# Four-head steps in latent attention, a later copy in the integer FFN, and a free bank for local attention's queries: one fused kernel on one core

## The chip, the core and the metric

The kernel runs on 1 core of one Trainium2 chip. Its time is device microseconds (us) from the start of the program to its end; less is better. The engines are TensorE (PE, with its weight loads shown as PEld), VectorE (DVE), ScalarE (ACT), GpSimd (POOL) and SyncE (SP, which only issues transfers here). They run side by side, each through its own list of instructions in order, and wait for one another on semaphores.

## The reference, cut to what matters

Four layers with float32 activations of 32 sequences x 256 tokens x 128 features; each layer is a layer norm, an attention branch `s`, an FFN branch `g`, and `x = x + s * silu(g)`. Three of the eight branches bear on the change:

```
# layer 0, attention: 8 query heads on 2 latent key/value heads, causal over 256 tokens
q = (x @ wq).reshape(Bq, Tq, N_KV, N_REP, HEAD_DIM)
k_lat = (x @ wk_down).reshape(Bq, Tq, N_KV, D_LAT)
v_lat = (x @ wv_down).reshape(Bq, Tq, N_KV, D_LAT)
scores = jnp.einsum('bqhrd,bkhd->bhrqk', q, k) * scale
probs = jax.nn.softmax(jnp.where(causal, scores, min), axis=-1)
y = jnp.einsum('bhrqk,bkhd->bqhrd', probs, v)
# layer 1, FFN: integer weights, hidden size 384
h = jax.nn.silu(x @ wg.T) * (x @ wu.T)
return h @ wd.T
# layer 3, FFN: two layers of windowed attention (8 heads of 64, window 64) and a gelu FFN
q, k = rotary_xpos(l2norm(q) * qs, l2norm(k) * ksc)
o = local_attention(q, k, v)
x = x + o @ wo
```

## The kernel before

Features lie on the 128 partitions, tokens along the rows. The program is a row of blocks; in each, every engine has a list written out in Python, and semaphores named after what was done (`scores`, `exps`, `turned_sb`) order the engines. `wait_ge(*S["exps"].at(i, n))` waits for the n-th exponential group of round i. PSUM is one tensor `ps` of 8 banks of 512 float32.

**Latent attention** (`latent_attention`) runs twice, for 16 sequences each, once with the transfers that scatter token rows to DRAM (`sorted_x`) and once with those that gather them. One sequence is four steps of two heads. A step's scores are three groups of matmuls into two banks (0 and 1, or 2 and 3 by turns): L573 and L576 are the score matmuls, each head in its own 32 rows of the array, L580 adds the causal mask. Then VectorE takes the row maxima (L750, L751), ScalarE the exponentials with their row sums (L712), TensorE turns the three 128-column blocks of each head (L589) into banks 4 and 5, VectorE copies them out (`probs_t`, L772), and `pe_mix` (L601) multiplies by the values into bank 6. Once a sequence come the reciprocals of the sums (L760), spread over the partitions by POOL (L677), TensorE (L611) and ScalarE (`inv_spread`, L724), the product `ot` (L765), the output projection (L623) with its copy (L739), and the projections k, q and v of sequences ahead (L617, L628), copied out by VectorE (k, L776) and ScalarE (q, L728, and v, L735). All of these use bank 7 in turn.

**Integer FFN** (`integer_ffn`): 16 chunks of 512 tokens, three hidden blocks f = 0, 1, 2 each. A step is a `down` matmul (L1312), one block of four transposes (L1288, L1296 or L1303, by f), an `up` matmul (L1323) and a `gate` matmul (L1328). Woven in is the next layer norm: `scale` (L1345) on ScalarE norms a chunk's rows, L1296 turns them back, and a ScalarE copy (L1360) puts them into `xn`; the silu of the gate (L1353) is ScalarE's too.

**Local attention** (`local_attention`), per layer 64 slots of 128 tokens. In slot k TensorE does the scores of k, the projections q and k of k + 3 and v of k + 1, transposes, the mix and the output of earlier slots. Seven of these results take banks 6 and 7 by turns, in the order of `MISC`; `pe_free` waits for whoever reads the result two places before. Bank 5 holds the mix (`attended` reads it), bank 4 the turned probabilities, banks 0 to 3 the scores.

Of the kernel before, what the change touches and what calls it, by code (L numbers as in the profile page):

```python
# [23 lines left out]
ALU = mybir.AluOpType  # L24
# [46 lines left out]
class Stage:  # L71
# [21 lines left out]
    "projected", "freed_act", "freed_dve", "scores", "masked", "rowmax", "exps", "turned", "turned_sb",  # L93
# [450 lines left out]
def latent_attention(nc, ps, m, w, first_pair, pairs, move, weights):  # L544
# [4 lines left out]
    with ExitStack() as mem:  # L549
# [5 lines left out]
        pr, nm, pt = buf("probs", P, 2, 2, W), buf("minus_max", P, 2, 2, 2), buf("probs_t", P, 4, 2, W)  # L555
# [7 lines left out]
        def pe_scores(pe, i, j):  # L563

            u, c, s = j % 8 // 4, j % 4 // 2, j % 2
            pe.wait_ge(*S["exps"].at(i, j - 2))
            if j % 4 == 0:
                pe.wait_ge(*S["k_sb"].at(i, j // 4))
                pe.wait_ge(*S["q_sb"].at(i, j // 4))
            b0 = 2 * s  # L570
            for e in range(2):
                rows = slice(32 * (2 * s + e), 32 * (2 * s + e) + 32)
                pe.matmul(ps[:, b0 + e, P:W], qt[rows, u, c, P:T], kt[rows, u, c, :], start=True, stop=False)  # L573
            for e in range(2):
                rows = slice(32 * (2 * s + e), 32 * (2 * s + e) + 32)
                pe.matmul(ps[:, b0 + e, 0:P], qt[rows, u, c, 0:P], kt[rows, u, c, 0:P], start=False, stop=False)  # L576
            for e in range(2):
                rows = slice(64 * e, 64 * e + 64)
                for h in range(2):
                    mm = pe.matmul(bank(ps, b0 + e, 3, P)[64 * h:64 * h + 64, ::2], one[rows, rows],  # L580
                                   hide[rows, h:h + 1].to_broadcast([64, 2, P]), start=False, stop=True)
            mm.then_inc(*S["scores"].inc)

        def pe_turn(pe, i, j):
            pe.wait_ge(*S["exps"].at(i, j))
            pe.wait_ge(*S["turned_sb"].at(i, j - 1))
            for e in range(2):
                for k in range(3):
                    mm = pe.transpose(ps[:, 4 + e, k * P:(k + 1) * P], pr[:, j % 2, e, k * P:(k + 1) * P], m["ident"][:])  # L589
            mm.then_inc(*S["turned"].inc)  # L590

        def pe_mix(pe, i, g):

            u, c = g % 4 // 2, g % 2
            pe.wait_ge(*S["turned_sb"].at(i, 2 * g + 1))
            pe.wait_ge(*S["v_sb"].at(i, g // 2))
            if c == 0:
                pe.wait_ge(*S["attended"].at(i, g // 2 - 1))
            for kb in range(2):
                for r in range(4):  # L600
                    mm = pe.matmul(ps[32 * r:32 * r + 32, 6, c * T + kb * P:(c + 1) * T], v[:, u, kb, c * LAT:(c + 1) * LAT],  # L601
                                   pt[:, (2 * g + r // 2) % 4, r % 2, kb * T:T + kb * P], start=(kb == 0), stop=(kb == 1))
            mm.then_inc(*S["mixed"].inc)

        def pe_spread(pe, i, n):
            pe.wait_ge(*S["widened"].at(i, n))
            if here(i, n + 2, 2):
                pe.wait_ge(*S["k_sb"].at(i, n + 2))
            for c in range(2):
# [22 lines left out]
        names = dict(copied=2, scores=8, rowmax=8, exps=8, turned=8, turned_sb=8, mixed=4, rowsum=2, widened=2, spread=2,  # L632
                     spread_sb=2, attended=2, q_ps=2, q_sb=2, k_ps=2, k_sb=2, v_ps=2, v_sb=2, o_ps=2, o_sb=2)
        with Stage(pairs, **names), Stage(1, moved0=TOK), nc.Block() as block:
            @block.tensor
            def _(pe):
                def body(i):
                    for t in range(8):
                        u, at = t // 4, t % 4
                        if t % 2 == 0 and here(i, t // 2 - 2, 4):  # L640
                            pe_mix(pe, i, t // 2 - 2)
                        if here(i, t + 1, 8):
                            pe_scores(pe, i, t + 1)
                        if here(i, t - 1, 8):
                            pe_turn(pe, i, t - 1)
                        if at == 0 and here(i, u - 1, 2):
                            pe_spread(pe, i, u - 1)
                        if at == 1 and here(i, u + 1, 2):
                            pe.wait_ge(*S["k_sb"].at(i, u + 1))
                            pe.wait_ge(*S["spread_sb"].at(i, u - 1))  # L650
                            pe_project(pe, i, u + 1, lambda c: wq[:, c], "q_ps")
                        if at == 2:
                            if here(i, u + 1, 2):
                                pe.wait_ge(*S["q_sb"].at(i, u + 1))
                            if here(i, u - 1, 2):
                                pe_out(pe, i, u - 1)
                            if here(i, u + 1, 2):
                                pe_v(pe, i, u + 1)
                        if at == 3 and here(i, u + 2, 2):
                            pe.wait_ge(*S["o_sb"].at(i, u - 1))  # L660
                            pe.wait_ge(*S["v_sb"].at(i, u + 1))
                            pe.wait_ge(*S["copied"].at(i, u + 2))
                            pe_project(pe, i, u + 2, lambda c: wk[:, c].rearrange("p r l -> p (r l)"), "k_ps")

                written_out(pairs, 1, 1, body)

            @block.gpsimd
            def _(pool):
# [3 lines left out]
                for i in range(-1, pairs + 1):  # L672
                    for u in range(2):
# [10 lines left out]
                        if here(i, u, 2):  # L684
                            for t in itertools.islice(tiles, TOK // (2 * pairs) - 1):
                                move(pool, t)
                            if here(i, u + 1, 2):
                                pool.wait_ge(*S["q_sb"].at(i, u + 1))
# [10 lines left out]
            def _(act):  # L699
                act.preload_act_table_set("exp_and_others")  # L700

                def exps(i, j):
                    u, c, s = j % 8 // 4, j % 4 // 2, j % 2
                    act.wait_ge(*S["rowmax"].at(i, j))
                    act.wait_ge(*S["turned"].at(i, j - 2))
                    if j % 4 == 0:
                        act.wait_ge(*S["rowsum"].at(i, j // 4 - 2))
                    for e in range(2):
                        head = 4 * c + 2 * s + e
                        for qb in range(2):  # L710
                            span = slice(qb * P, P + qb * T)
                            last = act.activation(pr[:, j % 2, e, span], ps[:, 2 * s + e, span], ACT.Exp,  # L712
                                                  bias=nm[:, s, qb, e:e + 1], accum_out=sums[:, u, qb, head:head + 1])
                    last.then_inc(*S["exps"].inc)

                def body(i):
                    for t in range(8):
                        u, at = t // 4, t % 4
                        if here(i, t, 8):
                            exps(i, t)  # L720
                        if at == 0 and here(i, u - 1, 2):
                            act.wait_ge(*S["spread"].at(i, u - 1))
# [1801 lines left out]
```

## Time and profile before

| | us |
|---|---|
| median of 3 runs (lowest to highest) | 2907.16 (2902.68 to 2909.36) |
| the profiled execution's own time | 2906.29 |
| its span in the trace | 2904.5 |
| TensorE busy | 2675.6 (92%) |
| VectorE busy | 2159.2 (74%) |
| ScalarE busy | 1934.7 (67%) |
| POOL busy | 1101.1 (38%) |

Busy time is the union of an engine's instructions in one profiled execution. Matmuls overlap in the array, so one that starts 0.05 us after another may last 0.2. A share over the whole span averages stages that differ, and what counts is read stage by stage. Times in the trace are us from the start of the span.

### The profile page before, as it was taken

Reading aid. Unit: us, or ns where it says so; the run is one execution under the profiler, and the core shown is the slowest. Engines: PE = TensorE matmul, PEld = TensorE weight load, DVE = VectorE, ACT = ScalarE, POOL = GpSimd, SP = SyncE. Lnnn points to the kernel's source line nnn. Section 1 sums busy time; section 2 is a strip of 40 time slices with the busy share of each in tenths; the row PEclk is TensorE's granted clock in tenths of the full one; section 3 lists DMA queues with packets and bytes.
Section 4 is the critical chain, followed back from the end, with each engine's and each line's share of the span. In section 5 each row is a group of like instructions: output and inputs, shape, how many; then the busy total and the mean of one; then the engine's idle time right before and its main releaser. Section 6 shows DMA issues by size and latency. Waiting matters only on the chain. (4 is left out here: it accounts for less than half of the span.)

```text
span 2904.5 us, 62166 instructions
## 1 busy us (share of the span) xinstructions
PE 2675.6 (92%) x21644; PEld 1785.4 (61%) x21644; DVE 2159.2 (74%) x3766; ACT 1934.7 (67%) x5521; POOL 1101.1 (38%) x1260
## 2 busy tenths in 40 slices
PE   7799999997889979888879999998998999999898
PEld 4577897774554434345547777776444777777644
DVE  4577565776675669856769999997447999999676
ACT  4366665666764544344369999997437999999744
POOL 0233343331004543310045555554215555555431
PEclk9699998998999989989989999999998999999999
DMA  4200121000000000030000000000000000000000
GB/s 147 77 23 21 52 68 30 22 22 12 9 17 0 1 0 1 10 74 9 20 9 2 2 2 2 2 2 10 12 1 10 2 2 2 2 2 2 2 22 37
DMA packets 83170, 53.92 MB, mean 19 GB/s; under 512 B 28848, under 2 KB 75568, under 8 KB 82864
## 3 DMA queue, kind: packets, MB, share of 16 engines
q1 hardware_dynamic: 78768, 41.56, 5.1%
q0 software_dynamic: 4096, 8.40, 1.0%
q8 instruction: 178, 2.92, 0.4%
q14 instruction: 128, 1.05, 0.1%
HBM read 31.59 MB, written 18.35 MB: 17 GB/s over the span
## 5 line engine op out<-in xcount | busy, mean ns | idle before, releaser
L2124 ACT ACTIVATE probs<-banks,minus_max,rnorm 128x128 f32<-128x128 f32 x1024 | 460.0, 469 | 4.3 <-DVE minus_max L2220 4.3
L1996 PE MATMUL banks<-weights,hf 128*128 128x512 f32 x768 | 431.1, 645 | 24.4 <-POOL hf L336 13.5
L2039 POOL TENSOR_TENSOR qk_cross<-qk_raw,rope_scaled 128x512 f32<-128x512 f32 x256 | 325.9, 1274 | 25.5 <-ACT qk_raw L2157 11.5
L2049 POOL TENSOR_TENSOR qk_rot<-qk_rot,rnorm 128x512 f32<-128x512 f32 x128 | 133.5, 1043 | 291.8 <-DVE qk_rot L2253 283.3
L2124 ACT ACTIVATION_READ_ACCUMULATOR probs<-banks,minus_max,rnorm 128x1 f32 x1024 | 222.6, 217 | 0.0
L712 ACT ACTIVATE probs<-banks,minus_max 128x128 f32<-128x128 f32 (+1 forms) x512 | 207.9, 425 | 13.1 <-DVE minus_max L751 13.1
L2200 DVE COPY probs_t<-banks 128x512 f32<-128x512 f32 x256 | 175.9, 687 | 54.5 <-PE banks L1974 53.9
L1974 PEld LDWEIGHTS banks<-ident,probs 128*128 128x128 f32 x1024 | 126.8, 140 | 134.4 <-issue 134.4
L2246 DVE TENSOR_TENSOR qk_rot<-qk_raw,rope_scaled 128x512 f32<-128x512 f32 x256 | 175.8, 727 | 0.0
L2234 DVE TENSOR_REDUCE sumsq<-qk_sq 128x16 f32<-128x1024 f32 x128 | 154.8, 1209 | 26.9 <-issue 19.9
L2005 PE MATMUL banks<-ident,qk_rot 128*128 128x128 f32 x1024 | 159.6, 279 | 10.0 <-DVE qk_rot L2253 4.9
L2253 DVE TENSOR_TENSOR qk_rot<-qk_rot,qk_cross 128x1024 f32<-128x1024 f32 x128 | 161.4, 1261 | 4.4
L2216 DVE TENSOR_REDUCE minus_raw<-banks 128x8 f32<-128x1024 f32 x128 | 155.5, 1215 | 7.6 <-PE banks L1966 7.6
L1974 PE MATMUL banks<-ident,probs 128*128 128x128 f32 x1024 | 153.9, 273 | 6.0 <-DVE probs_t L2200 5.8
L1996 PEld LDWEIGHTS banks<-weights,hf 128*128 128x128 f32 x768 | 117.8, 193 | 53.1 <-POOL hf L336 15.1
L2439 DVE SCALAR_TENSOR_TENSOR qk_rot<-banks,b1t,qk_rot 128x512 f32<-128x512 f32 x96 | 71.9, 749 | 104.9 <-ACT qk_rot L2392 91.0
L1988 PE MATMUL banks<-v_tok,probs_t 128*64 128x64 f32 x3072 | 148.7, 226 | 0.0
L2005 PEld LDWEIGHTS banks<-ident,qk_rot 128*128 128x128 f32 x1024 | 114.8, 142 | 42.2 <-issue 39.3
L1988 PEld LDWEIGHTS banks<-v_tok,probs_t 128*64 128x64 f32 x3072 | 130.9, 138 | 11.8 <-issue 10.2
L750 DVE TENSOR_REDUCE minus_max<-banks 128x2 f32<-128x256 f32 x128 | 54.4, 425 | 111.2 <-PE banks L580 111.2
L2090 PE MATMUL banks<-ot,weights 128*128 128x128 f32 x1024 | 135.5, 275 | 0.0
L2138 ACT ACTIVATE qk_sq<-qk_raw 128x1024 f32<-128x1024 f32 x128 | 134.2, 1048 | 0.1
(354 smaller groups left out, 6985.2 us busy)
## 6 DMA issues: line engine op xcount, KB each, us to landing
sorted_x<-zero_rows SPq DMA_DIRECT2D x10, 512.0 KB, 6.0
rows_in<-sorted_x SPq DMA_DIRECT2D x18, 256.0 KB, 3.1
sorted_y<-rows_out SPq DMA_DIRECT2D x18, 256.0 KB, 2.4
x_res<-in_x SPq DMA_DIRECT2D x8, 512.0 KB, 6.7
out_x<-x_res SPq DMA_DIRECT2D x16, 256.0 KB, 2.0
w1b<-in_L_ffn_w SPq DMA_DIRECT2D x8, 256.0 KB, 3.9
s_branch<-in_L_ffn_w SPq DMA_DIRECT2D x8, 256.0 KB, 5.8
w1g<-in_L_ffn_W SPq DMA_DIRECT2D x8, 256.0 KB, 3.0
```

The lines of the kernel that those rows point to most:

```text
L712: last = act.activation(pr[:, j % 2, e, span], ps[:, 2 * s + e, span], ACT.Exp, bias=nm[:, s, qb, e:e + 1], accum_out=sums[:, u, qb, head: ...
L1974: mm = pe.transpose(ps[:, 4, n * P:(n + 1) * P], pr[:, k % 2, 4 * h + n], m["ident"][:])
L1988: mm = pe.matmul(ps[64 * w:64 * w + 64, 5, at], pt[:, h, n * P + 64 * w:n * P + 64 * w + 64], vm[:, at] if tb and not w else va[:, k % 4, ...
L1996: pe.matmul(ps[:, misc(k, j)], hf[:, n // 2 % 2, 0, n % 2 * P:(n % 2 + 1) * P], wqkv[:, w:w + QW], start=True, stop=True).then_inc(*S[name ...
L2005: mm = pe.transpose(ps[:, misc(k, j), c * P:(c + 1) * P], st[:, n % 4, first:first + P], m["ident"][:])
L2039: return pool.tensor_tensor(by_half(tw[:, n, at]), by_half(qk[:, n, at])[:, :, ::-1, :], tab[:, n, 2 * w + 1].rearrange("p (a d) -> p a d" ...
L2124: last = act.activation(pr[:, k % 2, head], ps[:, 2 * (k % 2) + par, c * P:(c + 1) * P], ACT.Exp, scale=rn[:, k % 4, head:head + 1], bias= ...
L2200: dve.tensor_copy(pt[:, h], ps[:, 4]).then_inc(*S["turned_sb"].inc)
L2216: dve.tensor_reduce(nr[:].rearrange("p (b c) -> p b c", b=2), ps[:, 2 * (k % 2):2 * (k % 2) + 2].rearrange("p b (c t) -> p b c t", c=4), A ...
L2234: dve.tensor_reduce(ss[:], by_head(sq[:]), AX.X, ALU.add).then_inc(*S["sumsq"].inc)
L2246: last = dve.tensor_tensor(by_head(st[:, n, at]), by_head(qk[:, n % 2, at]), tab[:, n % 2, 2 * w:2 * w + 1].to_broadcast([P, HEADS, DH]), ...
L2253: dve.tensor_tensor(st[:, n], st[:, n], tw[:, n % 2], ALU.add).then_inc(*S["rotated"].inc)
```

## The change

Three edits in one.

1. *Latent attention* goes in steps (slots) of four heads. A slot fills banks 0 to 3 with one set of scores, each head in one of the four 32-row groups; the four heads' twelve blocks are turned in three groups of four, each a whole bank, and ScalarE copies the first (`lead_sb`), VectorE the other two. To make up, ScalarE takes the k copy, and VectorE those of `inv_spread`, v and s. POOL's transfers, three and then one per sequence, become one, two and one, with waits for `turned_sb` between them.
2. *Integer FFN*: ScalarE's copy of the normed rows to `xn` moves from f = 1 to f = 2, ahead of `scale`.
3. *Local attention*: q is projected into bank 5, between `attended` and the next mix, and is no longer in `MISC`, which has six entries now. Some waits that others imply are gone.

```diff
-        pr, nm, pt = buf("probs", P, 2, 2, W), buf("minus_max", P, 2, 2, 2), buf("probs_t", P, 4, 2, W)
+        pr, nm, pt = buf("probs", P, 2, 4, W), buf("minus_max", P, 2, 2, 2, 2), buf("probs_t", P, 2, 4, W)
...
+        def pe_scores(pe, i, g):
+
+            u, c = g % 4 // 2, g % 2
+            pe.wait_ge(*S["exps"].at(i, g - 1))
...
+            for r in range(4):
+                rows = slice(32 * r, 32 * r + 32)
+                pe.matmul(ps[:, r, P:W], qt[rows, u, c, P:T], kt[rows, u, c, :], start=True, stop=False)
...
+        def pe_turn(pe, i, g, t):
+            if t == 0 and not here(i, g + 1, 4):
+                pe.wait_ge(*S["exps"].at(i, g))
+            if t == 2:
+                pe.wait_ge(*S["lead_sb"].at(i, g))
+            else:
+                pe.wait_ge(*S["turned_sb"].at(i, 2 * (g - 1) + t))
+            for k in range(4):
+                mm = pe.transpose(ps[:, 4 + (g + t) % 2, k * P:(k + 1) * P], blocks(pr, g, t)[:, k * P:(k + 1) * P],
+                                  m["ident"][:])
             mm.then_inc(*S["turned"].inc)
...
+                            move(pool, next(tiles))
+                            if here(i, 2 * u - 1, 4):
+                                pool.wait_ge(*S["turned_sb"].at(i, 2 * (2 * u - 1) + 1))
+                            for t in itertools.islice(tiles, TOK // (2 * pairs) - 2):
                                 move(pool, t)
-                            if here(i, u + 1, 2):
-                                pool.wait_ge(*S["q_sb"].at(i, u + 1))
+                            pool.wait_ge(*S["turned_sb"].at(i, 2 * (2 * u) + 1))
                             move(pool, next(tiles))
...
+                    if here(i, g - 1, 4):
+                        act.wait_ge(*S["turned"].at(i, 3 * (g - 1)))
+                        act.wait_ge(*S["mixed"].at(i, g - 3))
+                        act.activation(blocks(pt, g - 1, 0), ps[:, 4 + (g - 1) % 2], ACT.Copy).then_inc(*S["lead_sb"].inc)
+                    if here(i, g, 4):
+                        exps(i, g)
...
                     if f == 0 and 0 <= c - 1 < R:
                         branch(c - 1)
+                    if f == 2 and 0 <= c - 3 < R:
+                        act.wait_ge(*S["copied"].at(0, c - 3))
+                        act.activation(m["xn"][:, tokens(c - 3)], ps[:, ROWS_AT], ACT.Copy).then_inc(*S["normed"].inc)
                     if f == 2 and 0 <= c - 2 < R:
                         scale(c - 2)
-                    if f == 1 and 0 <= c - 3 < R:
-                        act.wait_ge(*S["copied"].at(0, c - 3))
-                        act.activation(m["xn"][:, tokens(c - 3)], ps[:, ROWS_AT], ACT.Copy).then_inc(*S["normed"].inc)
...
-MISC = [("qt_sb", 1), ("added", -3), ("q_sb", 3), ("kt_sb", 1), ("k_sb", 3), ("v_sb", 1), ("ot_sb", -2)]
-QT_AT, OUT_AT, Q_AT, KT_AT, K_AT, V_AT, OT_AT = range(7)
+MISC = [("qt_sb", 1), ("added", -3), ("kt_sb", 1), ("k_sb", 3), ("v_sb", 1), ("ot_sb", -2)]
+QT_AT, OUT_AT, KT_AT, K_AT, V_AT, OT_AT = range(6)
...
+        def pe_project_q(pe, i, k):
+            n = k + 3
+            if here(i, k - 2):
+                pe.wait_ge(*S["attended"].at(i, k - 2))
+            else:
+                pe.wait_ge(*S["q_sb"].at(i, n - 1))
+            pe.wait_ge(*S["copied"].at(i, n // 2))
+            pe.matmul(ps[:, 5], hf[:, n // 2 % 2, 0, n % 2 * P:(n % 2 + 1) * P], wqkv[:, 0:QW], start=True, stop=True)\
+                .then_inc(*S["q_ps"].inc)
```

In the middle of latent attention TensorE's list was, for somewhat more than two heads (`kt,qt` are the scores, `hide` the masks, `probs` the transposes, `v_tok` the mix, `wk_lat` and `wq_lat` projections):

```order
L573 MATMUL banks<-kt,qt 128x256 x2
L576 MATMUL banks<-kt,qt 128x128 x2
L580 MATMUL banks<-hide,ident_bf 64x2x128 x4
L589 MATMUL banks<-ident,probs 128x128 x6
L617 MATMUL banks<-xf,wk_lat 128x256 x2
L601 MATMUL banks<-probs_t,v_tok 32x256 x4
L601 MATMUL banks<-probs_t,v_tok 32x128 x4
```

Of the change, one slot and the start of the next:

```order
L575 MATMUL banks<-kt,qt 128x256 x4
L578 MATMUL banks<-kt,qt 128x128 x4
L583 MATMUL banks<-hide,ident_bf 64x2x128 x8
L595 MATMUL banks<-ident,probs 128x128 x4
L623 MATMUL banks<-ident,inv_wide 128x128 x4
L595 MATMUL banks<-ident,probs 128x128 x8
L629 MATMUL banks<-xf,wq_lat 128x256 x2
L609 MATMUL banks<-probs_t,v_tok 32x256 x4
L609 MATMUL banks<-probs_t,v_tok 32x128 x4
```

Scores come once for four heads instead of twice, and the transposes in fours. ScalarE's list in the same place, of the change, with the semaphores each row waits for (L743 copies q, L747 is the new copy of the first turned bank, L731 the exponentials):

```order
L743 ACTIVATE qt<-banks 128x512 [waits q_ps]
L747 ACTIVATE probs_t<-banks 128x512 [waits mixed,turned]
L731 ACTIVATE probs,row_sums<-banks,minus_max 128x128 [waits rowmax,turned]
L731 ACTIVATE probs,row_sums<-banks,minus_max 128x256
L731 ACTIVATE probs,row_sums<-banks,minus_max 128x128
L731 ACTIVATE probs,row_sums<-banks,minus_max 128x256
L731 ACTIVATE probs,row_sums<-banks,minus_max 128x128 [waits rowmax]
```

The copy of the turned bank stands between a slot's scores and its exponentials. In the integer FFN, ScalarE's list for one chunk before:

```order
L1353 ACTIVATE silu_gate<-banks 128x512
L1338 ACTIVATE gate<-banks 128x512
L1365 ACTIVATE s_branch<-banks,weights 128x512
L1353 ACTIVATE silu_gate<-banks 128x512
L1360 ACTIVATE xn<-banks 128x512
L1353 ACTIVATE silu_gate<-banks 128x512
L1345 ACTIVATE ln_rows<-banks,ln_shift,ln_scale 128x128 x4
```

And of the change:

```order
L1376 ACTIVATE silu_gate<-banks 128x512
L1361 ACTIVATE gate<-banks 128x512
L1388 ACTIVATE s_branch<-banks,weights 128x512
L1376 ACTIVATE silu_gate<-banks 128x512 x2
L1381 ACTIVATE xn<-banks 128x512
L1368 ACTIVATE ln_rows<-banks,ln_shift,ln_scale 128x128 x4
```

The third silu has moved ahead of the copy to `xn`. In local attention, TensorE's projections q, k and v of one slot before, with what they wait for and what stands between them:

```order
L1996 MATMUL banks<-weights,hf 128x512 [waits copied,qt_sb]
L1974 MATMUL banks<-ident,probs 128x128 [waits turned_sb,exps]
L2005 MATMUL banks<-ident,qk_rot 128x128 [waits unit,added]
L1996 MATMUL banks<-weights,hf 128x512 [waits copied,q_sb]
L1996 MATMUL banks<-weights,hf 128x512 [waits copied,kt_sb]
```

And of the change:

```order
L2023 MATMUL banks<-weights,hf 128x512 [waits copied,attended]
L1995 MATMUL banks<-ident,probs 128x128 [waits exps]
L2038 MATMUL banks<-ident,qk_rot 128x128 [waits unit,qt_sb]
L2029 MATMUL banks<-weights,hf 128x512 [waits added]
L2029 MATMUL banks<-weights,hf 128x512 [waits kt_sb]
```

The order of the work is the same; q waits for the reader of bank 5, k for the reader of the output, v as before.

## Rows read from the trace of the kernel before

**Rows 1.** Stretches of the span, busy us (instructions): PE, PEld, DVE, ACT, POOL; clock.

```profile
478.00:486.00 8.00, 8.00 (x42) 6.50 (x43) 3.57 (x6) 4.48 (x21) 0.94 (x1) 0.50 0.03 8
486.00:657.00 171.00, 171.00 (x1695) 129.78 (x1695) 122.30 (x205) 111.56 (x487) 65.53 (x83) 1.00 0.09 23
1600.00:1900.00 300.00, 298.81 (x3642) 220.52 (x3639) 281.15 (x431) 284.00 (x898) 174.13 (x180) 1.00 0.01 2
```

**Rows 2.** Time line, latent attention, TensorE: start, us, engine, line, instructions.

```profile
212.21 0.70 PE L573 MATMUL banks<-kt,qt 32*128 32x256 f32 x4
213.06 0.30 PE L580 MATMUL banks<-hide,ident_bf 64*64 64x256 bf16 x4
213.30 0.88 PE L589 MATMUL banks<-ident,probs 128*128 128x128 f32 x6
...
214.97 0.86 PE L601 MATMUL banks<-probs_t,v_tok 128*32 128x256 f32 x16
215.76 0.70 PE L573 MATMUL banks<-kt,qt 32*128 32x256 f32 x4
```

**Rows 3.** The same time line, VectorE and ScalarE; in brackets idle time before.

```profile
213.42 0.42 DVE L750 TENSOR_REDUCE minus_max<-banks 128x2 f32<-128x256 f32 x1 [0.44 <-PE banks L580]
213.76 0.68 DVE L751 TENSOR_REDUCE minus_max<-banks 128x2 f32<-128x512 f32 x1
214.36 0.95 DVE L772 COPY probs_t<-banks 128x768 f32<-128x768 f32 x1
215.07 0.60 ACT L728 ACTIVATE qt<-banks 128x512 f32<-128x512 f32 x1 [0.55 <-PE banks L617]
215.57 0.36 ACT L712 ACTIVATE probs<-banks,minus_max 128x128 f32<-128x128 f32 x1
...
219.49 0.37 ACT L712 ACTIVATE probs<-banks,minus_max 128x128 f32<-128x128 f32 x1
...
222.67 0.21 ACT L712 ACTIVATION_READ_ACCUMULATOR probs<-banks,minus_max 128x1 f32 x1
```

**Rows 4.** Time line, first latent stage: its first and fourteenth `ot`, its last copy.

```profile
127.97 0.69 DVE L765 TENSOR_TENSOR ot<-banks,inv_spread 128x512 f32<-128x512 f32 x1 [0.59 <-PE banks L601]
...
291.25 0.69 DVE L765 TENSOR_TENSOR ot<-banks,inv_spread 128x512 f32<-128x512 f32 x1 [0.59 <-PE banks L601]
...
311.91 0.38 ACT L739 ACTIVATE s_branch<-banks 128x256 f32<-128x256 f32 x1 [2.70 <-PE banks L623]
```

**Rows 5.** Integer FFN: time line of one chunk; last, waits (total, times, longest).

```profile
932.61 1.02 PE L1312 MATMUL banks<-hid,w_deq 128*128 128x512 f32 x2
933.47 0.60 PE L1296 MATMUL banks<-ident,ln_rows 128*128 128x128 f32 x4
933.91 1.02 PE L1323 MATMUL banks<-xn,w_deq 128*128 128x512 f32 x2
934.11 0.60 ACT L1360 ACTIVATE xn<-banks 128x512 f32<-128x512 f32 x1 [4.08 <-PE banks L1296]
...
935.24 1.13 PE L1328 MATMUL banks<-xn,w_deq 128*128 128x512 f32 x2 [0.31 <-ACT silu_gate L1353]
...
943.73 0.60 ACT L1360 ACTIVATE xn<-banks 128x512 f32<-128x512 f32 x1 [4.08 <-PE banks L1296]
...
PE banks L1328 <- ACT silu_gate L1353: 3.8, 12, 0.3
```

**Rows 6.** Time line, local attention, one slot: projections and the copies they wait for.

```profile
1702.13 0.60 ACT L2133 ACTIVATE qt<-banks 128x512 f32<-128x512 f32 x1
...
1702.82 1.08 PE L1996 MATMUL banks<-weights,hf 128*128 128x512 f32 x2
...
1703.74 0.60 PE L1974 MATMUL banks<-ident,probs 128*128 128x128 f32 x4
...
1705.30 0.60 ACT L2153 ACTIVATE kt<-banks 128x512 f32<-128x512 f32 x1
...
1705.99 1.09 PE L1996 MATMUL banks<-weights,hf 128*128 128x512 f32 x2
```

More of the change, by code:

```diff
@@ L561, in here @@
             return there(i, n, per, pairs)
[L563 to L589, printed above, removed]
+        def blocks(x, g, t):
+            return x[:, g % 2].rearrange("p h w -> p (h w)")[:, 4 * t * P:4 * (t + 1) * P]
+        def pe_scores(pe, i, g):
+            u, c = g % 4 // 2, g % 2
+            pe.wait_ge(*S["exps"].at(i, g - 1))
+            if c == 0:
+                pe.wait_ge(*S["k_sb"].at(i, g // 2))
+                pe.wait_ge(*S["q_sb"].at(i, g // 2))
+            for r in range(4):
+                rows = slice(32 * r, 32 * r + 32)
+                pe.matmul(ps[:, r, P:W], qt[rows, u, c, P:T], kt[rows, u, c, :], start=True, stop=False)
+            for r in range(4):
+                rows = slice(32 * r, 32 * r + 32)
+                pe.matmul(ps[:, r, 0:P], qt[rows, u, c, 0:P], kt[rows, u, c, 0:P], start=False, stop=False)
+            for s in range(2):
+                for e in range(2):
+                    rows = slice(64 * e, 64 * e + 64)
+                    for h in range(2):
+                        mm = pe.matmul(bank(ps, 2 * s + e, 3, P)[64 * h:64 * h + 64, ::2], one[rows, rows],
+                                       hide[rows, h:h + 1].to_broadcast([64, 2, P]), start=False, stop=True)
+                mm.then_inc(*S["scores"].inc)
@@ L667, in _ @@
+                written_out(pairs, 1, 1, lambda i: [slot(i, g) for g in range(4)])
             @block.gpsimd
@@ L744, in _ @@
+                written_out(pairs, 1, 1, lambda i: [slot(i, g) for g in range(4)])
             @block.vector
             def _(dve):
[L746 to L752 removed]
@@ L778, in _, with rowmax, turned @@
-                written_out(pairs, 1, 1, body)
+                def rowmax(i, g, s):
+                    dve.wait_ge(*S["scores"].at(i, 2 * g + s))
+                    dve.wait_ge(*S["exps"].at(i, g - 2))
+                    for qb in range(2):
+                        last = dve.tensor_reduce(nm[:, g % 2, s, qb], ps[:, 2 * s:2 * s + 2, qb * P:P + qb * T], AX.X,
+                                                 ALU.max, negate=True)
+                    last.then_inc(*S["rowmax"].inc)
+                def turned(i, g, t):
+                    dve.wait_ge(*S["turned"].at(i, 3 * g + t))
+                    if t == 1:
+                        dve.wait_ge(*S["mixed"].at(i, g - 2))
+                    dve.tensor_copy(blocks(pt, g, t), ps[:, 4 + (g + t) % 2]).then_inc(*S["turned_sb"].inc)
@@ L779, in latent_attention @@
+                written_out(pairs, 1, 1, lambda i: [slot(i, g) for g in range(4)])
         S["loaded"].base += 16 * len(weights)
```

215 lines of the change are left out of this document (103 added, 112 removed).

## The prediction

> **What bounds the kernel now.** I read the table of stretches first, then the time line inside each of the three stages that the diff touches, then the waits. The three stages are bound in three different ways.
>
> Latent attention (two stages of 16 sequences each). In a steady stretch of 171.00 us TensorE is busy for 171.00 us at the full granted clock, 2.4 GHz [rows 1]. The multiplication `ot` comes 13 intervals after its first occurrence at 291.25, so one sequence takes (291.25 - 127.97) / 13 = 12.56 us [rows 4]. For two heads TensorE needs 1.09 us for the scores (212.21 to 213.30), of which 0.85 are the score matmuls and the rest the masks; six transposes take 0.88 to their end; `pe_mix` takes 0.79 (214.97 to 215.76) [rows 2]. VectorE waits for TensorE here [rows 3], and ScalarE is busy for 111.56 of the 171.00 us [rows 1]. So only TensorE's instructions count.
>
> Integer FFN. Here the bound is a stall, not work. ScalarE stands 4.08 us in front of its copy to `xn`, waiting for the transposes of L1296; the silu that is queued behind the copy comes late, and TensorE's next gate matmul, which could start at 933.91 + 0.86 = 934.77, starts at 935.24 [rows 5]. A 512-column float32 matmul takes 0.86 (932.61 to 933.47) and a block of four transposes 0.44 (933.47 to 933.91), so a chunk is 9 x 0.86 + 3 x 0.44 = 9.06 us of TensorE, and its period is 943.73 - 934.11 = 9.62 [rows 5]. The loss is 0.56 a chunk, and TensorE was caught by that silu 12 times [rows 5].
>
> Local attention (two layers of 64 slots). TensorE is busy 298.81 of 300 us, VectorE 281.15, ScalarE 284.00 [rows 1]. All three are nearly full, so only small things are to be had. The q projection takes 0.92 (1702.82 to 1703.74), where the same matmul takes 0.86 elsewhere [rows 6, 5]: it waits for ScalarE's copy `qt`, which ends at 1702.13 + 0.60 = 1702.73, and comes with no time left to load the second half of the weights ahead.
>
> **The change, part by part: latent attention.** The four heads of a step now sit in four row groups, so what ran twice for two heads runs once for four. Scores for four heads cost 1.09 plus the second set of masks, which I put at 0.11 (an estimate: half of the 0.21 that 256 of the 0.86 us' 512 columns take in one of two passes, since the masks are bfloat16), 1.20 instead of 2.18. That is 0.98 per slot off TensorE, about 2 us of the 12.56 per sequence, and it ceases to be the bound.
>
> What is late next: the score banks are no longer doubled. All four are filled by one step, so `pe_scores` of slot g waits for the last exponential of slot g - 1, and behind that wait the whole TensorE queue stands. The ring, counted from the first score matmul: VectorE's first reduction starts at 1.21 (212.21 to 213.42) [rows 2, 3]; two reductions end at 1.21 + 0.34 + 0.68 = 2.23 [rows 3]. ScalarE meanwhile has the new `lead` copy: its four transposes start at 1.20 and end some 0.66 later (0.88 for six), so it starts near 1.89, and the next ScalarE instruction comes 0.50 behind such a copy (215.07 to 215.57) [rows 2, 3]. The exponentials therefore start at 2.39, not at 2.23. Four heads of them take 222.67 + 0.21 - 219.49 = 3.39 [rows 3], until 5.78, and a hand-over to TensorE about 0.05 to 0.1: **5.87 a slot**. A second ring goes through VectorE: 1.21, four reductions (2 x (0.34 + 0.60) = 1.88, as consecutive starts stand), then the copy of `inv_spread`, now VectorE's (0.60), two `probs_t` copies (0.60 and, to the end, 0.68), 0.05, and the mix with its 0.79 in front of the next scores: 5.81 [rows 2, 3]. In the other slot v and s (the shorter copies) replace that one. Both rings lie so close that one waits for the other now and then; I take 5.9, 11.8 a sequence, 0.76 less than now.
>
> Over 13 intervals that is 9.9 a stage. The end gives some back. Now the stage ends 311.91 + 0.38 - 291.25 = 21.04 after its last regular `ot` [rows 4]; after the change three slots follow that point (17.5 to the last exponential), and then transposes, lead copy, third transposes, copy, mix, `ot`, projection and copy in a row, 6.8: 24.3, so 3.2 worse. The start I leave at nothing: TensorE does less, but in the first two slots it must wait some 3 us for exponentials. There it ran at a granted 0.50 (1.2 GHz) though never idle [rows 1], and I can't read when the clock rises; bounds plus and minus 3. Sum: 9.9 - 3.2 = 6.7 a stage, **13.4** for two.
>
> What the trace does not show is four row groups at once. Two at once cost no more than one would ([rows 2]: the second of a pair hides). Bounds: 0, or, if the groups go two by two, the 0.85 again less the change of tile shape, about 0.75 a slot. Four column groups at once, in the mix, take 0.79 for eight matmuls [rows 2]; that is nearest in kind, so I take 0. The Trainium skill ("TensorE: Matmul & The Clock Gate", Part 3, measured speedup against the span model) gives four row tiles 3.07 times one, not four; the four would take 1.30 times one, and by that the slot would be an estimated 6.1 and the forecast 2891 instead of 2879. No row here shows four, so it is a rival below.
>
> The spread transfers (POOL) I cost at nothing: POOL is busy 65.53 of 171.00 us with its moves and copies [rows 1], and the only thing that waits for it is `pe_spread`, through `inv_wide`, which comes after 1.2 us of scores and four transposes. Where a move is still running then, that cover is gone, and a slot grows by up to one POOL instruction, 65.53 / 83 = 0.79 us on the mean [rows 1].
>
> **Integer FFN.** The copy now follows the silu of f = 2, so ScalarE's wait for L1296 holds up only the copy and `scale`, which has to wait for `ln_shift` anyway. The silu has its gate long before, and TensorE finds `act_a` done. Period 9.06: 12 x 0.56 = 6.7; I take **6.5**. Behind the copy `scale` now starts 0.5 after the transposes' end, and the next chunk's silu follows with about 2 us to spare for its `down` matmul. That cover hides it.
>
> **Local attention.** Nothing is added or taken out; q moves from banks 6 and 7 to bank 5, and waits. The q projection waits for `attended` (VectorE, long done) instead of the `qt` copy: 0.92 becomes 0.86, **0.06 a slot**. The k projection waited for the q copy, and now waits for `added` instead. I give that nothing: the v projection still waits for the `kt` copy (1705.30 + 0.60 = 1705.90, v starts 1705.99) [rows 6], which stands on ScalarE behind the q copy and two exponentials, as before. What k gains, v waits longer. 0.06 x 124 full slots = **7.4**. Bounds: 0, if another ring (VectorE is 94% full [rows 1]) takes over, and 0.18 a slot, 22, if k and v have an excess of the same size and both lose it.
>
> **Sum.** 13.4 + 6.5 + 7.4 = 27.3 off the profiled execution's own 2906.29 us, which is 0.87 below the median: 2879.
>
> **The rivals.** *Four row groups overlap only in part* (their weight loads stand in line): a quarter of the 0.75 between the bounds, 0.2 more a slot. A stage has about 29 slots that count (13 x 2 + 3), so 5.8 a stage and 2891. For it: four groups load eight weights where two load four. Against it: the mix loads for four groups within its 0.79 [rows 2]. The rule of the Trainium skill above (Part 3 of that page) would make this the likely case; the trace bears out only pairs.
>
> *Two by two*, the case on the other side: slot 5.87 + 0.75 = 6.6, 29 x 0.7 = 20 a stage more than forecast, 41 in all: 2920, slower. It decides from a slot of 6.4 on, where latent attention loses what the other two parts gain. Against it: tiles in other shapes run four at a time here.
>
> *The two small edits do nothing*: the FFN's stall turns up behind `scale`, and VectorE's ring binds local attention. 2879 + 14 = 2893. For it: VectorE and ScalarE are 94% and 95% busy there [rows 1]. Against it: the FFN's stall is one wait with one cause.
>
> *More than forecast*: k's and v's excess in local attention falls too, 15 more, 2864; or the start of latent attention gains 3 a stage.
>
> **How the numbers follow.** Forecast 0.50 (its own range 2868 to 2889), partial overlap 0.18, small edits nothing 0.08, more 0.14, two by two 0.07, the rest a mixture near no change. What is within 0.2% (5.8 us) can't be told from no change. Faster by more: 0.87; same 0.05; slower 0.08. From 2857 to 2897 the first four cases are nearly all held, with the bounds of the start and of local attention.
>
> **What would show it.** Right: `ot` every 11.8 us; TensorE about 90% busy in latent attention and waiting before the scores for ScalarE's `probs`; the `xn` copy's wait no longer followed by a late silu, chunks at 9.06; q at 0.86, v still above 0.9, slots 0.06 shorter. Wrong: scores for four heads much above 1.2, or a long wait for VectorE's `probs_t` in front of the mix, either of which makes the slot longer than 6.1; a `kt` copy that comes earlier than I reckon; or half clock reaching into the steady part.

## The result, and the profile after

2865.93 us (median of 4 runs, 2861.49 to 2867.06), against 2905.41 for the kernel before: a ratio of 0.9861, 95% interval 0.9848 to 0.9874. The time fell by some 40 us where 27 were forecast; the profiled spans are 2904.5 and 2864.5. The 40 us, read from how much earlier the same instruction starts in the two traces:

| part | forecast | measured |
|---|---|---|
| latent attention, up to the first `ot` | 0 (plus and minus 3 a stage) | -3.4 and -5.3 |
| latent attention, 13 intervals | -9.9 a stage | -10.3 and -10.0 |
| latent attention, end | +3.2 a stage | +4.6 and +4.0 |
| integer FFN | -6.5 | -7.1 |
| local attention, first slots (a layer's first projection to its fifth `qt` copy) | not looked at | -4.9 and -5.8 |
| local attention, full slots (from there to the last `qt` copy) | -7.4 for both layers | -1.6 and -1.8 |
| local attention, ends | not looked at | +1.7 and +1.0 |

Minus is faster. The rest, about 1, is small differences between the stages.

**Latent attention.** The time line of VectorE has the first and the fourteenth `ot` and the last copy of both stages:

```profile
124.53 0.69 DVE L779 TENSOR_TENSOR ot<-banks,inv_spread 128x512 f32<-128x512 f32 x1 [1.06 <-PE banks L609]
...
277.50 0.69 DVE L779 TENSOR_TENSOR ot<-banks,inv_spread 128x512 f32<-128x512 f32 x1 [1.06 <-PE banks L609]
...
302.67 0.42 DVE L795 COPY s_branch<-banks 128x256 f32<-128x256 f32 x1 [1.22 <-PE banks L635]
...
478.54 0.69 DVE L779 TENSOR_TENSOR ot<-banks,inv_spread 128x512 f32<-128x512 f32 x1 [1.06 <-PE banks L609]
...
631.83 0.69 DVE L779 TENSOR_TENSOR ot<-banks,inv_spread 128x512 f32<-128x512 f32 x1 [1.06 <-PE banks L609]
...
656.44 0.42 DVE L795 COPY s_branch<-banks 128x256 f32<-128x256 f32 x1 [1.91 <-PE banks L635]
```

(277.50 - 124.53) / 13 = 11.77 a sequence, where [rows 4] give 12.56; 25.6 from the last regular `ot` to the end, where it was 21.04. One slot on TensorE and ScalarE:

```profile
212.63 0.71 PE L575 MATMUL banks<-kt,qt 32*128 32x256 f32 x8
213.17 0.40 PE L578 MATMUL banks<-kt,qt 32*128 32x128 f32 x8
213.50 0.41 PE L583 MATMUL banks<-hide,ident_bf 64*64 64x256 bf16 x8
213.84 0.66 PE L595 MATMUL banks<-ident,probs 128*128 128x128 f32 x4
...
214.54 0.60 ACT L747 ACTIVATE probs_t<-banks 128x512 f32<-128x512 f32 x1 [1.57 <-PE banks L595]
...
215.03 0.36 ACT L731 ACTIVATE probs<-banks,minus_max 128x128 f32<-128x128 f32 x1
...
218.10 0.25 ACT L731 ACTIVATION_READ_ACCUMULATOR probs<-banks,minus_max 128x1 f32 x1
...
218.53 0.71 PE L575 MATMUL banks<-kt,qt 32*128 32x256 f32 x8
```

Scores of four heads take 213.84 - 212.63 = 1.21; the exponentials start 2.40 behind the first score (forecast 2.39), and the next scores come after 5.90. Eight score matmuls in four row groups take 0.71 where four in two take 0.70 [rows 2]. From two groups to four nothing is lost. One group alone stands in no row. With half of the 0.86 of a 512-column matmul [rows 5], 0.43, as an estimate for one, four in 0.54 (212.63 to 213.17) would be 3.2 times one. The Trainium skill ("TensorE: Matmul & The Clock Gate", Part 3, measured speedup against the span model) gives 3.07 times for four row tiles; the estimate is near it, and no run here tests it.

**The granted clock** by stretches of latent attention's second start and steady part, the integer FFN and local attention (columns as in [rows 1]):

```profile
450.30:463.70 13.40, 11.38 (x44) 7.03 (x44) 2.24 (x5) 3.75 (x9) 3.82 (x6) 0.50 0.06 15
463.70:467.10 3.40, 1.05 (x21) 0.82 (x24) 0.00 (x0) 2.88 (x13) 0.00 (x0) 0.99 0.00 0
467.20:470.60 3.40, 3.40 (x23) 3.11 (x16) 2.60 (x6) 1.96 (x8) 0.00 (x0) 0.50 0.02 5
...
470.00:640.00 170.00, 157.28 (x1792) 118.76 (x1792) 121.17 (x244) 123.46 (x519) 68.79 (x86) 1.00 0.09 24
905.00:965.00 60.00, 60.00 (x200) 30.35 (x199) 42.20 (x158) 31.09 (x64) 38.76 (x41) 1.00 0.00 1
1570.00:1870.00 300.00, 298.25 (x3672) 218.30 (x3671) 283.51 (x432) 284.97 (x901) 174.08 (x181) 1.00 0.01 2
```

TensorE now waits in latent attention (157.28 of 170.00) and is full in the integer FFN. There the copy still waits, and delays no silu: the chunk is 938.37 - 929.33 = 9.04, forecast 9.06.

```profile
929.33 0.60 ACT L1381 ACTIVATE xn<-banks 128x512 f32<-128x512 f32 x1 [3.71 <-PE banks L1319]
...
938.37 0.60 ACT L1381 ACTIVATE xn<-banks 128x512 f32<-128x512 f32 x1 [3.71 <-PE banks L1319]
```

**Local attention, a full slot** on TensorE, from the q projection to the v projection:

```profile
1668.59 1.02 PE L2023 MATMUL banks<-weights,hf 128*128 128x512 f32 x2
1669.45 0.60 PE L1995 MATMUL banks<-ident,probs 128*128 128x128 f32 x4
1669.89 0.60 PE L2038 MATMUL banks<-ident,qk_rot 128*128 128x128 f32 x4
1670.33 1.02 PE L2029 MATMUL banks<-weights,hf 128*128 128x512 f32 x2
1671.19 0.60 PE L1995 MATMUL banks<-ident,probs 128*128 128x128 f32 x4
1671.67 1.13 PE L2029 MATMUL banks<-weights,hf 128*128 128x512 f32 x2
1672.63 0.38 PE L2140 MATMUL banks<-ident,attended_tok 128*128 128x128 f32 x2
```

q takes 1669.45 - 1668.59 = 0.86 (0.92 before), as forecast. k takes 1671.19 - 1670.33 = 0.86 (0.94 before), but the turn behind it 0.48 (0.44 before), and v 0.96 (0.93 before): what k gains v waits, as forecast. Starts of the `qt` copy, before (the one behind that of [rows 6], and the next) and after:

```profile
1710.55 0.60 ACT L2133 ACTIVATE qt<-banks 128x512 f32<-128x512 f32 x1
1718.87 0.60 ACT L2133 ACTIVATE qt<-banks 128x512 f32<-128x512 f32 x1
...
1667.90 0.60 ACT L2165 ACTIVATE qt<-banks 128x512 f32<-128x512 f32 x1 [0.17 <-PE banks L2038]
1676.26 0.60 ACT L2165 ACTIVATE qt<-banks 128x512 f32<-128x512 f32 x1 [0.19 <-PE banks L2038]
1684.58 0.60 ACT L2165 ACTIVATE qt<-banks 128x512 f32<-128x512 f32 x1 [0.16 <-PE banks L2038]
```

They stand 8.36 and 8.32 apart by turns, where it was 8.42 and 8.32: every second slot gained nothing.

### The profile page after: what moved, and what is told of

Its sections match the earlier page's. It is cut to its first block and busy times, and to the rows that moved or that the text cites. A ratio compares the mean times of both kernels' runs of the same rounds, so it can differ in the third digit from the quotient of the medians.

```text
span 2864.5 us, 61209 instructions
## 1 busy us (share of the span) xinstructions
PE 2606.9 (91%) x21644; PEld 1734.9 (61%) x21644; DVE 2145.7 (75%) x3830; ACT 1946.8 (68%) x5521; POOL 1103.3 (39%) x1260
## 5 line engine op out<-in xcount | busy, mean ns | idle before, releaser
L2029 PE MATMUL banks<-weights,hf 128*128 128x512 f32 x512 | 276.8, 623 | 5.0 <-ACT kt L2185 5.0
L731 ACT ACTIVATE probs<-banks,minus_max 128x128 f32<-128x128 f32 (+1 forms) x512 | 206.6, 437 | 5.2 <-DVE minus_max L759 5.0
L759 DVE TENSOR_REDUCE minus_max<-banks 128x2 f32<-128x256 f32 (+1 forms) x256 | 124.9, 551 | 61.6 <-PE banks L583 61.6
L2023 PE MATMUL banks<-weights,hf 128*128 128x512 f32 x256 | 135.2, 611 | 13.6 <-POOL hf L336 13.6
```

Of the source, the lines that this page charges most:

```text
L731: last = act.activation(pr[:, g % 2, 2 * s + e, span], ps[:, 2 * s + e, span], ACT.Exp, bias=nm[:, g % 2, s, qb, e:e + 1], accum_out=sums[ ...
L2029: pe.matmul(ps[:, misc(k, j)], hf[:, n // 2 % 2, 0, n % 2 * P:(n % 2 + 1) * P], wqkv[:, w:w + QW], start=True, stop=True).then_inc(*S[name ...
```

## The experiments

A kernel's ratio is to the kernel before, run on the same chip.

**One part at a time** (three kernels: before, with the diff's part and nothing else).

> The kernel before with only the integer FFN's copy moved. Theory: the stall of 0.56 us a chunk is gone, chunks come every 9.06, and the time falls by 6.5 to 8 us against the kernel before (ratio about 0.9975). Rival: the stall turns up again behind the copy, chunk at 9.62 or near it, no change. The starts of the local layers should show TensorE's clock rising as in the kernel before, some 20 us after the layer's first matmuls; if it rises much earlier here too, the rise differs from one execution to the next and is no effect of the change.

0.9974 (0.9964 to 0.9984). From the integer FFN's end on its trace is 7 us ahead; its local layers start as before, first intervals of the `qt` copy 8.05, 7.61 and 8.16 (8.23, 7.61 and 8.16 in the kernel before).

> The kernel before with only local attention's part. Theory A: half of the slots gain 0.05 to 0.06 us (q at 0.86) and the other half, which POOL's two copies to v_mixed hold at 8.32, gain nothing: 1.75 us a layer, 3.5 in all, and the clock rises earlier at the start of both layers, 3.6 and 5.7 us more: 2905 - 12.5 = 2893. Theory B: the earlier rise is chance; then 3.5 alone, 2902. Theory of the prediction: 0.06 in every slot, 7.4, 2898.

0.9966 (0.9954 to 0.9978), 9.9 us. The interval rules out theory B, but holds A's 12.5 and the prediction's 7.4; the slots are A's: first intervals 6.40, 7.25, 7.51, then 8.36 and 8.32. A's reason for the starts, the clock, is put to the test in the next run but one.

> The kernel before with only latent attention's part. Theory A: 13 intervals x 0.79 = 10.2 a stage less, the end 4 to 4.5 worse, the start 3.4 and 5.3 better because TensorE's clock rises sooner: about 20 less in all, 2885. Theory B: the earlier rise is chance or comes from elsewhere: 12 less, 2893. In both, one sequence takes 11.77.

0.9937 (0.9923 to 0.9950), 18 us: theory A in size (20), and B's 12 is outside. The three parts add up to 0.9877, just above the interval of the whole (0.9848 to 0.9874); with their own intervals the two agree.

**q waits again, in bank 5.**

```diff
                 pe.wait_ge(*S["attended"].at(i, k - 2))
             else:
                 pe.wait_ge(*S["q_sb"].at(i, n - 1))
+            if here(i, k + 1):
+                pe.wait_ge(*S["qt_sb"].at(i, k + 1))
```

> The changed kernel, in which the q projection stays in bank 5 but waits for ScalarE's copy of the turned queries again. Theory: the gain of a slot comes from the wait alone and not from the bank: q goes back to 0.92 us, the slots that had 8.36 go to 8.42, and the time rises by 3 to 4 us to about 2869.5. If the bank itself were worth something, q would stay at 0.86 or the time would not rise. The starts of the layers keep their earlier rise of the clock, since in the first slots the wait is not there.

0.9904 (0.9889 to 0.9919): by the ratios 12 us of the gain gone, not 3 to 4. Full slots are at 8.43 and 8.33, as expected, but the first layer's first intervals are back at 8.64, 7.63, 8.17, for this wait is there in the first slots too. TensorE there, second and third slot of the first layer:

```profile
1451.97 0.66 PE L2040 MATMUL banks<-ident,qk_rot 128*128 128x128 f32 x4
1453.36 1.10 PE L2025 MATMUL banks<-weights,hf 128*128 128x512 f32 x2 [0.73 <-issue]
...
1458.78 0.66 PE L2040 MATMUL banks<-ident,qk_rot 128*128 128x128 f32 x4
1461.01 1.10 PE L2025 MATMUL banks<-weights,hf 128*128 128x512 f32 x2 [1.57 <-issue]
```

And in the changed kernel:

```profile
1452.82 0.66 PE L2038 MATMUL banks<-ident,qk_rot 128*128 128x128 f32 x4
1453.31 1.02 PE L2023 MATMUL banks<-weights,hf 128*128 128x512 f32 x2
...
1459.23 0.66 PE L2038 MATMUL banks<-ident,qk_rot 128*128 128x128 f32 x4
1459.84 1.10 PE L2023 MATMUL banks<-weights,hf 128*128 128x512 f32 x2
```

In a full slot eight output matmuls (0.89) stand between the query transposes and q, and cover the copy `qt`. In a layer's first slots there is no output yet, and q stands until the copy is done, 0.73 and 1.57 here. So most of the gain of the starts is this wait: from a layer's first projection to its fifth `qt` copy the kernel before takes 44.64 and 45.35, the change 39.73 and 39.59, and this run 43.51 and 42.71. It is not the whole. The first copy comes 10.62 and 11.09 behind the first projection in this run too (10.63 and 10.62 in the change, 12.22 and 12.23 before); and the clock has a part in the second layer, as the next run shows.

**q waits in full slots only** (the same, with `here(i, k - 3) and` ahead of the condition).

> The changed kernel, in which the q projection waits for ScalarE's copy of the turned queries only from the fourth slot of a layer on, where an output matmul stands between the two. Theory: the first slots keep their 3.4 to 5 us a layer (first intervals 6.4, 7.2, 7.5 as in the change), the full slots lose 0.06 and 0.01 by turns, 2 us a layer: 4 us slower than the change, ratio to before 0.9875. Rival (the gain of the starts is the clock's and comes and goes): the first intervals of a layer are not those of the change, ratio 0.990 or 0.986.

0.9878 (0.9861 to 0.9894). Time, full slots (8.43 and 8.33) and the first layer's first intervals (6.51, 7.24, 7.51) are as the theory has them. The second layer's are 7.35, 7.24 and 7.51, where the change has 6.30, 7.23 and 7.51: there the rival has a part. Its first 18 us, in the change and in this run (columns as in [rows 1]):

```profile
2150.50:2168.50 18.00, 13.55 (x68) 6.75 (x69) 9.84 (x12) 8.97 (x17) 9.29 (x9) 0.83 0.00 1
...
2148.70:2166.70 18.00, 14.62 (x61) 6.90 (x62) 8.22 (x11) 8.12 (x15) 8.83 (x9) 0.65 0.00 1
```

The waits of these slots are the same; the mean granted clock is 0.83 in one and 0.65 in the other, and up to the fifth `qt` copy they take 39.59 and 41.12. The second layer of the run with local attention alone takes 41.13. So some 1.5 of the 5.8 that the second layer's start gained go with the clock of the one execution, and not with the wait.

**The lead copy on VectorE.**

```diff
-                        act.activation(blocks(pt, g - 1, 0), ps[:, 4 + (g - 1) % 2], ACT.Copy).then_inc(*S["lead_sb"].inc)
...
                     if here(i, g - 1, 4):
+                        dve.tensor_copy(blocks(pt, g - 1, 0), ps[:, 4 + (g - 1) % 2]).then_inc(*S["lead_sb"].inc)
                         turned(i, g - 1, 1)
```

> The changed kernel, in which VectorE and not ScalarE copies the first of the three turned banks in latent attention. Theory: both engines' rings were close (5.87 and 5.81 us a slot); without the copy ScalarE's ring is 5.71, but VectorE's has one more copy of 0.60, 6.4 in the slots with the copy of the spread sums and about 6.3 in the others; so ot comes every 12.7 us in place of 11.77, and with 29 slots a stage the time rises by some 28 us, 2894. Rival (ScalarE's ring alone decides): a slot loses the 0.17 by which the copy delays the exponentials, ot every 11.4, 10 us faster, 2856.

1.0047 (1.0031 to 1.0064): 53 us slower than the change, `ot` every 13.45. The sign is the theory's, the size is not. From the time line of one slot:

```profile
211.15 0.71 PE L575 MATMUL banks<-kt,qt 32*128 32x256 f32 x8
...
213.51 0.37 ACT L731 ACTIVATE probs<-banks,minus_max 128x128 f32<-128x128 f32 x1 [2.48 <-DVE minus_max L755]
...
214.84 0.68 DVE L796 COPY probs_t<-banks 128x512 f32<-128x512 f32 x1
...
215.58 0.66 PE L595 MATMUL banks<-ident,probs 128*128 128x128 f32 x4 [1.69 <-DVE probs_t L796]
...
216.27 0.69 DVE L763 COPY probs_t<-banks 128x512 f32<-128x512 f32 x1 [0.15 <-PE banks L595]
...
217.11 0.86 PE L609 MATMUL banks<-probs_t,v_tok 128*32 128x256 f32 x16
```

Without ScalarE's copy the exponentials start 2.36 behind the scores, with it 2.40: where it stands it costs 0.04, not the 0.16 of the forecast. VectorE's first two reductions end 2.25 behind the scores here, as forecast (2.23), but the exponentials start 0.12 after them, a hand-over that the forecast left out. And the copy has a price that I had left out: the third group of transposes reuses its bank, so copy, transposes, copy and mix stand in a row.

**POOL's transfers as before, three and one.**

```diff
-                            move(pool, next(tiles))
...
-                            for t in itertools.islice(tiles, TOK // (2 * pairs) - 2):
+                            for t in itertools.islice(tiles, TOK // (2 * pairs) - 1):
                                 move(pool, t)
-                            pool.wait_ge(*S["turned_sb"].at(i, 2 * (2 * u) + 1))
+                            if here(i, u + 1, 2):
+                                pool.wait_ge(*S["q_sb"].at(i, u + 1))
                             move(pool, next(tiles))
```

> The changed kernel, with POOL's transfers in latent attention as before the change, three and then one. Theory of the prediction: the spread of the transfers is worth nothing, since inv_wide has 1.2 us of scores and four transposes as cover; ot every 11.77, 2866 within 3 us. Rival: three moves in a row hold inv_wide or the copy of the tokens back, by up to one move (0.95 us) a sequence: 32 x 0.95 = 30 slower at most.

0.9855 (0.9839 to 0.9872) and `ot` every 11.77, as in the change, whose ratio it can't be told from: the spread is worth nothing, as forecast.

**Who holds every second slot at 8.32?** In the changed kernel, VectorE and POOL in such a slot:

```profile
1679.43 0.60 POOL L2099 COPY v_mixed<-v_tok 64x512 f32<-64x512 f32 x1 [0.16 <-POOL qk_cross L2072]
...
1680.08 0.61 POOL L2100 COPY v_mixed<-v_tok 64x512 f32<-64x512 f32 x1
...
1680.31 0.42 DVE L2268 TENSOR_SCALAR sumsq<-sumsq 128x16 f32<-128x16 f32 x1
...
1680.63 0.68 DVE L2232 COPY probs_t<-banks 128x512 f32<-128x512 f32 x1
```

A VectorE instruction on 16 columns takes 0.42 and ends, at 1680.73, when POOL's copy does (1680.69); in the other slots it takes 0.17. The Trainium skill ("SBUF — State Buffer", Who interferes with whom) has such a rule for some VectorE instructions, `tensor_scalar` among them: the two engines share a pair of ports, and the second to come waits for the whole instruction of the first. These rows agree. Three runs on it, the first:

```diff
                 def slot(i, k):
+                    if here(i, k + 2):
...
+                        cross(i, k, 0)
                     if here(i, k + 1):
                         heads = by_head(st[:, (k + 1) % 4, QW:])
```

> The changed kernel, with POOL's first qk_cross of a slot put ahead of its product with rnorm, into the 2.3 us that POOL idles a slot. Theory: in every second slot the chain of POOL's work (product, two crosses, two copies to v_mixed, 5.24 us from VectorE's last product of one slot) holds VectorE's small tensor_scalar until POOL's last copy ends, and so the slot at 8.32; with the chain 1.3 shorter these slots become shorter than 8.30, bound as the others, and up to 0.06 x 62 = 3.7 us go, 2862. Rival: the cross now lies beside VectorE's two long products and slows them by 0.2 to 0.3 a slot: 124 x 0.25 = 31 slower.

0.9992 (0.9982 to 1.0002), 38 us slower than the change: the rival. Every second slot takes 8.93, for two VectorE products beside the moved cross take 2.13 in place of 1.28:

```profile
1668.45 2.13 DVE L2279 TENSOR_TENSOR qk_rot<-qk_raw,rope_scaled 128x512 f32<-128x512 f32 x2
```

In the second, the block of the two copies stands ahead of that of the two crosses:

```diff
+                        pool.tensor_copy(vm[0:64], va[0:64, k % 4])
+                        pool.tensor_copy(vm[64:128], va[64:128, k % 4 - 1]).then_inc(*S["v_mixed"].inc)
...
                         cross(i, k, 0)
```

> The changed kernel, with POOL's two copies to v_mixed ahead of its two crosses. Theory, as in the run with the cross first: VectorE's small tensor_scalar of the odd slots is no longer held by the copies but by the end of the second cross, 0.1 to 0.2 earlier; slots of 8.32 become 8.26 to 8.30, up to 3.7 us faster. Rival (POOL doesn't hold these slots, something else does): 8.32 stays.

0.9874 (0.9858 to 0.9891), slots of 8.36 and 8.33 still. It tells nothing apart, and my expectation was at fault: POOL's work in the slot is as long in either order, and now the second cross held the same instruction (0.42).

```diff
-                        pool.tensor_copy(vm[0:64], va[0:64, k % 4])
-                        pool.tensor_copy(vm[64:128], va[64:128, k % 4 - 1]).then_inc(*S["v_mixed"].inc)
+                        pool.tensor_copy(vm[0:64, 0:128], va[0:64, k % 4, 0:128])
+                        pool.tensor_copy(vm[64:128, 0:128], va[64:128, k % 4 - 1, 0:128]).then_inc(*S["v_mixed"].inc)
```

> The changed kernel, in which POOL's two copies to v_mixed move only 128 of their 512 columns, so that every second slot's mix works on a part of the values only. Theory: POOL's chain of 5.24 us from VectorE's last product of one slot to the end of the copies becomes 0.8 shorter, VectorE's small tensor_scalar in that slot takes 0.17 in place of 0.42, and the slots of 8.32 become 8.1 to 8.26, bound by TensorE's own work or by VectorE: 62 x 0.06 to 0.2 a layer pair, 4 to 13 us less. Rival (something else sets these slots): 8.32 stays.

0.9841 (0.9825 to 0.9858); slots of 8.36 and 8.25:

```profile
1674.63 0.29 POOL L2101 COPY v_mixed<-v_tok 64x128 f32<-64x128 f32 x1
...
1675.17 0.17 DVE L2269 TENSOR_SCALAR sumsq<-sumsq 128x16 f32<-128x16 f32 x1
```

So POOL's chain held these slots. The slots show it and not the time, whose interval overlaps that of the change.

**Versions that use it.** POOL's copies become transfers from SyncE (shown for `v_mixed`):

```diff
+                            sp.wait_ge(*S["v_sb"].at(i, k))
+                            sp.wait_ge(*S["mixed"].at(i, 2 * (k - 2) + 1))
+                            sp.dma_start(vm[0:64], va[0:64, k % 4]).then_inc(*S["fetched0"].inc)
+                            sp.dma_start(vm[64:128], va[64:128, k % 4 - 1]).then_inc(*S["fetched0"].inc)
...
-                        pool.tensor_copy(vm[0:64], va[0:64, k % 4])
-                        pool.tensor_copy(vm[64:128], va[64:128, k % 4 - 1]).then_inc(*S["v_mixed"].inc)
```

> The changed kernel, in which transfers issued by SyncE, not POOL, copy the two halves of v_mixed, with the whole computation done. Theory: as with a quarter of the copies, the slots of 8.32 become 8.25 or less (TensorE's own work or VectorE), 8.36 stays; 2.3 us a layer, 4 to 5 us faster than the change, 2861, ratio to before about 0.9845. Rival: the transfer lands later than POOL's copy and the mix waits for it, the same or slower.

2862.23 us, 0.9849 (0.9835 to 0.9862); slots of 8.36 and 8.25, as expected. By its time alone it can't be told from the change.

```diff
+                            sp.wait_ge(*S["v_ps"].at(i, k + 1))
...
+                            sp.dma_start(hf[0:64, k // 2, 0, :], m["xn"][0:64, first:first + T])\
...
-                        shift_in(pool, hf[:, k // 2], m["xn"], i, 0, T, S["v_ps"].at(i, k + 1), first=first)
```

> The same, and also the shifted rows hf come by transfers. Theory: in the slots of 8.36 VectorE's two products beside POOL's copies to hf took 1.48 and 1.30 instead of 1.28 and 1.23; without these copies VectorE's ring is 0.2 to 0.27 shorter there, and TensorE's own instructions (8.1 to 8.2 a slot) or ScalarE's ring bind: 8.15 to 8.25 in all slots, 62 x 0.1 to 0.2 more a layer than with v_mixed alone: 2840 to 2850, ratio 0.978 to 0.982. Rival: the transfers are seen by TensorE too late (issued when v is projected, wanted by q some 4.4 us later), slots of over 8.36.

2854.89 us, 0.9829 (0.9816 to 0.9843), the fastest kernel here, and faster than the change beyond both intervals. All slots are at 8.25 but a few, at the slow end of what was expected, and the time lies some 5 us above the expected 2840 to 2850. TensorE is busy throughout:

```profile
1640.00:1850.00 210.00, 209.67 (x2567) 153.81 (x2566) 192.20 (x304) 201.12 (x633) 90.60 (x77) 1.00 0.11 25
```

## Why the prediction was right, and where it was off

The direction, the time (inside the stated range, 2 us below the likeliest case's own) and the main mechanisms held; four terms were mis-sized. That the sum came so near is in part luck. The starts of latent attention (8.7) and the first slots of local attention (10.7) were put at nothing or not looked at; local attention's full slots (4.0), latent attention's ends (2.2) and the layers' ends (2.7) fell short of the forecast and made up for about half of it. The rival *more than forecast* names 2864, near what was measured, but k's and v's excess, its main reason, did not go: v stands at 0.96.

*Latent attention, steady part*: right, 11.77 against 11.8. Four row groups cost as much as two, so neither "partial overlap" nor "two by two" came. The ring through ScalarE had the right length, 5.90 for 5.87, with two wrong steps in it: the lead copy is hidden behind the reductions and their hand-over, and the hand-over to TensorE, put at 0.05 to 0.1, takes 0.18 (218.10 + 0.25 to 218.53).

*Its start*, put at nothing: 3.4 and 5.3 better, the second outside the bound of 3. The step that failed is "TensorE does less, but must wait". Before, at a granted 0.50, five sets of scores stood ahead of the first mix of the second stage, 1.94 us each (466.77 to 468.71); now it is two, of 2.16 and 1.35 us, and from the first projection to the first mix it takes 471.71 - 450.52 = 21.2 where it took 486.61 - 460.14 = 26.5. A set of scores that is saved at half clock is worth 1.94 and not the 1.09 of [rows 2]; TensorE's wait of 2.35 in there doesn't eat that up. No run tests this by itself; that the start gains was named among the rivals, with 3 a stage.

*Its end*, put at 3.2: 4.6 and 4.0. The step is the row of dependent work behind the last exponential, reckoned at 6.8: it takes 7.3 in the first stage (295.80 to 303.09) and 7.7 in the second. That row left out VectorE's copy of `inv_spread`, which stands right ahead of its last `probs_t` copies (297.81, then 298.41); how much of the difference it makes no run shows. In the first stage the last exponential also ends 18.3 behind the last regular `ot` and not 17.5; the granted clock was 0.50 there from 289.70 to 293.10, which may be why.

*Integer FFN*: right, 9.04 for 9.06.

*Local attention*: the local term of 7.4 took all of 124 slots as one kind. The full slots gave 3.4, since in every second one POOL's chain, and not TensorE, sets the time (shown by `v_mixed_quarter`); I had read VectorE's 94% as a bound and not what VectorE waited for inside its own instructions. That the k projection's gain passes to v held.

The first slots gave 10.7, because the wait that I had measured behind its cover (0.06) is bare there: put back in `q_waits`, it takes 3.8 and 3.1 of the 4.9 and 5.8. Ahead of the first `qt` copy the change gains 1.6 a layer, of which `q_waits` keeps 1.6 and 1.1. There, before, TensorE stood 0.69 twice behind copies of earlier projections (ahead of its matmuls at 1467.90 and 1472.37), and in the change the same projections run one behind the other; that is read from the traces, and no run tests it. Some 1.5 of the second layer's gain go with the clock, as said. What the layers' ends gave back I didn't test.

## What to carry to other kernels

A wait is priced where its cover is thinnest: look at the first and last rounds of a pipeline, where the instructions that hide it in the middle are missing. When slots alternate between two lengths, they have two bounds; find both before the saving is multiplied by all of them. And a short instruction that takes several times its usual time next to another engine's work is a wait that no list of waits shows.

## What the runs showed of the hardware

The granted clock can be high while TensorE has little to do, and low while it is full: in latent attention's second start it was 1.2 GHz for 13.4 us with TensorE busy 11.38, then 2.4 GHz for 3.4 us in which TensorE was busy 1.05, and, behind those, 1.2 GHz again for 3.4 us of full work (the first three rows of stretches above). The run with latent attention alone has the same pattern (0.68 of 3.2 us busy at full clock, then 3.20 of 3.20 at half), so it repeats. At the start of local attention's second layer, kernels that do the same there differ: a mean granted 0.83 in one and 0.65 in another, and 1.5 us in time.

A VectorE instruction on 8 columns with two inputs takes 0.47 where POOL's cross runs, and 0.17 in the run with the cross moved away from it; the products on 512 columns are slowed too (2.13 for 1.28).
